# SyncE's order of issue in an attention kernel: weight and residual loads moved between the quarters of the exchange

## What is computed

```python
xn = layernorm(x)                                   # x: 2048 x 512, float32
q = (xn @ wq.T)                                     # 16 heads of 128 + 64 (rotary)
kv_lat, k_pe = split(xn @ wkv_a.T)                  # 128 latent, 64 rotary
q_lat = einsum(q_nope, wkv_b[:, :128]); q_pe, k_pe = rope(q_pe), rope(k_pe)
kv_cache = rmsnorm(kv_lat, kv_norm_w)
scores = (q_lat @ kv_cache.T + q_pe @ k_pe.T) * SCALE    # causal
out = softmax(scores) @ kv_cache @ wkv_b[:, 128:] @ wo.T
return x + out + xn @ ternary(weight).T + bias
```

## Time and profile before

| | |
|---|---|
| median of 3 runs | 1836.02 us (1835.36 to 1843.37) |
| the profiled execution | 1835.36 us, of it the span 1833.3 us |
| TensorE busy | 1715.3 us (94%) |
| VectorE, ScalarE, GpSimd busy | 1211.6, 849.0, 1009.4 us |
| granted TensorE clock, mean | 0.976 |
| SyncE's DMA queue, share of 16 engines | 43.7% |
| ScalarE's DMA queue | 15.8% |
| mean of all DMA traffic | 169 GB/s |

### The profile page before, as it was taken

One profiled execution on the slowest core, in us unless ns is written; L12 is line 12 of the kernel. 1 busy time (PEld: TensorE's weight loads), 2 busy tenths in 40 slices (PEclk: granted clock), 3 DMA queues, 4 the chain that ended last, 5 costly groups with the idle time before them and its releaser, 6 DMA issues. The chain is left out here.

```text
span 1833.3 us, 28210 instructions
## 1 busy us (share of the span) xinstructions
PE 1715.3 (94%) x9326; PEld 1446.9 (79%) x9326; DVE 1211.6 (66%) x2801; ACT 849.0 (46%) x1358; POOL 1009.4 (55%) x635
## 2 busy tenths in 40 slices
PE   6999789888999999999999999989999999999996
PEld 5887577667777777778888888878888888888885
DVE  4765476656666776666676666767677666766763
ACT  4554344443444544444544445434544544554442
POOL 4674544443555555555556556554646555565654
PEclk9888899989999999999999999999999999999998
DMA  6995355563766656756555545565756565655553
GB/s 196 371 331 212 107 148 171 161 216 110 202 172 167 160 151 179 210 167 172 150 149 154 157 132 149 170 188 151 191 132 151 146 164 130 158 153 130 149 129 109
DMA packets 127680, 309.12 MB, mean 169 GB/s; under 512 B 29554, under 2 KB 42099, under 8 KB 126388
## 3 DMA queue, kind: packets, MB, share of 16 engines
q1 hardware_dynamic: 98784, 227.04, 43.7%
q10 hardware_dynamic: 28756, 80.35, 15.8%
HBM read 113.28 MB, written 34.60 MB: 81 GB/s over the span
## 5 line engine op out<-in xcount | busy, mean ns | idle before, releaser
L1416 POOL TENSOR_TENSOR pT<-pT,pT_h 128x1024 fp32r<-128x1024 f32 x320 | 689.3, 2184 | 415.2 <-ACT pT_h L1322 413.2
L1196 DVE TENSOR_SCALAR_CACHE_REDUCE probs<-p_score 128x512 f32<-128x512 f32 (+3 forms) x640 | 382.2, 603 | 371.7 <-PE p_score L1124 225.9
L1301 ACT ACTIVATE probs<-probs,neg_max 128x128 f32<-128x128 f32 (+15 forms) x256 | 307.6, 1202 | 449.7 <-DVE neg_max L1202 399.4
L1322 ACT ACTIVATE pT_h<-pT 128x1024 fp32r<-128x1024 f32 x320 | 291.2, 963 | 241.9 <-PE p_out L1144 175.1
L1218 DVE STREAM_TRANSPOSE turned<-probs 128x1024 f32<-128x1024 f32 (+7 forms) x384 | 341.8, 916 | 40.6 <-ACT probs L1301 36.1
L1144 PE MATMUL p_out<-pT_h,V_h 128*128 128x256 f32 (+3 forms) x1024 | 301.3, 294 | 22.7 <-POOL pT L1416 22.6
L1144 PE MATMUL p_out<-pT,V_h 128*128 128x256 f32 (+3 forms) x1024 | 303.2, 296 | 0.0
L1144 PE MATMUL p_out<-pT_h,V_l 128*128 128x256 f32 (+3 forms) x1024 | 302.8, 296 | 0.0
L1124 PE MATMUL p_score<-Kp,qp_h 128*128 128x512 f32 (+3 forms) x640 | 236.8, 370 | 16.8 <-POOL qp_l L1408 16.7
L1124 PE MATMUL p_score<-Kn_h,q_h 128*128 128x512 f32 (+3 forms) x640 | 241.2, 377 | 3.5 <-DVE q_l L1241 3.0
L1124 PE MATMUL p_score<-Kn_l,q_h 128*128 128x512 f32 (+3 forms) x640 | 234.5, 366 | 0.0
(11 more groups left out here) (135 smaller groups left out, 2348.4 us busy)
## 6 DMA issues: line engine op xcount, KB each, us to landing
pT<-turned SPq DMA_DIRECT2D x384, 128.0 KB, 3.5
Wq<-wq_scr ACTq DMA_DIRECT2D x63, 512.0 KB, 4.4
Wv<-wv_scr SPq DMA_DIRECT2D x63, 512.0 KB, 3.8
pT<-turned SPq DMA_DIRECT2D x192, 112.0 KB, 3.8
pT<-turned SPq DMA_DIRECT2D x192, 96.0 KB, 2.6
pT<-turned ACTq DMA_DIRECT2D x128, 128.0 KB, 3.9
Wp<-wp_scr SPq DMA_DIRECT2D x31, 512.0 KB, 4.8
pT<-turned SPq DMA_DIRECT2D x192, 80.0 KB, 2.8
```

The source lines that it names most:

```text
L1196: dve.tensor_scalar(probs[row % ROW_RING][:, b * CW:b * CW + width], p_score[n % SCORE_RING][:, 0:width], SCALE, LOWEST, ALU.mult, ALU.max ...
L1301: act.activation(probs[row % ROW_RING][:, 0:width], probs[row % ROW_RING][:, 0:width], ACT.Exp, bias=neg_max[p][:, i:i + 1], scale=1.0, ac ...
L1322: act.activation(high.rearrange("p r t i q -> p r t (i q)"), low.bitcast(F32).rearrange("p r t i q -> p r t (i q)"), ACT.Copy).then_inc(p_ ...
L1416: pool.tensor_tensor(low.rearrange("p r t i q -> p r t (i q)"), low.bitcast(F32).rearrange("p r t i q -> p r t (i q)"), high.bitcast(F32). ...
```

## The change

Only the order of calls in SyncE's `slot(s)` is changed. No DMA is added, removed or resized, and each keeps its own waits. In every slot `load_rotary`, so far last, now stands between quarters 1 and 2 of the exchange and ahead of `load_next_v`. In the slots of a chunk change the second `store_half` and both `load_residual` now stand between the quarters.

```diff
                 if new:
                     store_half(new - 1, 0)
-                if new and new > 1:
-                    store_half(new - 1, 1)
                 if 1 <= s <= SLOTS:
-                    exchange(s - 1, (0, 1))
-                if s < 2 * H:
-                    load_next_v(s)
-                if new == 1:
+                    exchange(s - 1, (0,))
+                if new:
                     store_half(new - 1, 1)
                     load_residual(new, 0)
                 if 1 <= s <= SLOTS:
-                    exchange(s - 1, (2,))
-                if new and new > 1:
-                    load_residual(new, 0)
+                    exchange(s - 1, (1,))
                 if new:
                     load_residual(new, 1)
+                if opens_head(s) and head_of(s) % 2 and head_of(s) + 3 < HEADS:
+                    load_rotary(head_of(s) + 3)
+                if s < 2 * H:
+                    load_next_v(s)
+                if 1 <= s <= SLOTS:
+                    exchange(s - 1, (2,))
                 if s >= 2 * H:
                     load_next_v(s)
-                if opens_head(s) and head_of(s) % 2 and head_of(s) + 3 < HEADS:
-                    load_rotary(head_of(s) + 3)
```

## The result

The changed kernel takes 1869.18 us in the median (4 runs, 1862.61 to 1871.96), the kernel before in the same comparison 1839.69 us (4 runs): ratio 1.0155, 95% interval 1.0124 to 1.0186, or +29.5 us. It is slower, and it lies 13 us above the upper end of the predicted range. Sixteen further runs of the changed kernel have a median of 1868.7 us (1855.4 to 1874.8). In later comparisons the kernel before had medians of 1839.85 (29 runs), 1840.75 (23) and 1842.83 (28). One of these 28, at 3302.26 us, was a slow execution, and the intervals leave it out. So the execution profiled before (1835.36) was a favourable one; that of after took 1873.42 us, of it the span 1871.3. The two traces therefore differ by 38.0 us where the medians differ by 29.5.

The account below looks back on a forecast made before the run. Bound taken: exchange and `Wv` landing just in time in chunk 1, and tight chunk changes. Terms -1.0 + 2.9 + 0.8 + 1.0 + 3.3 + 1.7 = +8.7 us on 1835.36 gave 1844.1, median 1844.7 us, range 1837 to 1856.

Parts of the forecast that it names:

- The `Wp` loads: Chunk 0: issue hidden in a wait, -1.0 us; chunk 1: quarter 2 later, +2.9; slot 29: `Wv` later, +0.8.
- The row named as the sign of it: Chunk 1: TensorE's waits at L1156 were to go up; no size given.
- The second and third change: Slots 35 and 67: quarter 2 lands late behind store and residual, +3.3 us (0.2 to 5.7) and +1.7 (0 to 3.6).
- The wait: Slots 35 and 67: second residual half waits 5.9 us for the second store's landing, with quarter 2 behind it.
- The size: Quarter 2 lands 4.6 us late in slot 35 and 2.1 in slot 67, of which 1.3 and 0.4 are covered.
- The price per transfer that I held in hand: Chunk 1: upper bound of 2.1 us, the distance at which two such loads land under load.
- The first change: Slot 18: quarter 2 costs the loop 1.0 us, `Wv` some 4 us late, half swallowed; +1.0 us, bounds 0 and 4.
- The figure of 1.5 us: Chunk 1, `Wv` behind `Wp`: estimated time of 512 KB at 358 GB/s; 1.7 us was taken instead.
- The loop pays for the whole of `Wp`: Rival, odd slots 17 to 29: quarter 2 is 2.1 us late per slot, roundings 10.4 in all; 1852.2 us, chance 0.22.
- Hidden: Rival, whole kernel: every delay at its lower end, stores landing in 3 us; +0 to +4 us, about 1838, chance 0.23.
- faster: Rival, slot 18 and chunk 0: earlier loads end waits, -4 us at most, 1832; chance 0.05 of over 0.5% faster.

## Why the prediction was wrong

**What bounds the kernel** was read rightly: exchange and `Wv` arrive at their use in chunk 1, and the chunk changes are tight. The signs of the three terms for the chunk changes and of the sum for `Wp` came out, nothing was lost elsewhere in chunks 2 and 3, and slots 36 and 68 were the ones named. The times of issue were right to within 1 us too: in slot 18 `Wv` was expected 9.1 us after quarter 0 and went out at 8.8, in slot 35 quarter 2 was to be out at 11.5 and was at 10.7. What was wrong is what came between issue and landing. The loss was predicted at +8.7 and is +29.5.

**The `Wp` loads**, terms -1.0, +2.9 and +0.8, together +2.7: measured +5.7 (interval 1.7 to 9.8), so the term is in bounds. Measured from the start of quarter 0, quarter 2 lands in the odd slots 21 to 29 after 17.0 us in the mean (15.4 before), which is 1.6 later where 1.0 was taken, and `Wv` 1.4 later where 1.7 was taken. The whole set of traces agrees: the six with `Wp` last in the slot (before among them) have 15.0 to 16.1 us, the six with `Wp` ahead 16.5 to 17.9. In chunk 0 it lands no earlier, and the gain of 1.0 isn't seen. Where in chunk 1 the time is paid I can't show. The row named as the sign of it, the projection's wait for "issue" from 455 to 800 us, is 2.3 us in before and 10.5 with `Wp` moved:

```profile
PE p_result L1157 <- issue: 10.5, 8, 2.6
```

But the kernel with only the store moved in slots 35 and 67 has 11.0 there, with the old order in every slot of that stretch:

```profile
PE p_result L1159 <- issue: 11.0, 7, 2.4
```

and four others with `Wp` last in the slot have 3.3 to 6.6. A trace of one execution doesn't decide it.

**The second and third change**, +3.3 and +1.7: this is the step that failed. Slots 36 and 68 grew by 9.7 and 9.4 (7.0 to 9.7 and 5.5 to 9.4 over three kernels of that order). Three things were wrong in it.

- The wait. "The second residual half waits for its landing, 5.9 us" didn't occur: behind a store issued 5.0 us earlier, SyncE was still issuing quarter 1 when it had landed, and with the store done early and only the residual between, slot 36 still grew by 6.6.
- The size. I let quarter 2 be late by its later issue and a little sharing: 4.6 and 2.1 us. In truth 1.5 MB were put ahead of it in the same queue while the engines were full, and it was 8.3 and 7.8 us late, up to 2.8 us for each transfer (6.1 to 8.3 and 4.3 to 7.8 over the four kernels of that order). The price per transfer that I held in hand, up to 2.1 us, was near for one (1.8 and 1.9 measured) but was used nowhere in this step. Three times 2.1 would have given 6.3 and a term of +5.0.
- The clock. No term for it. A stall of 2.5 to 6.8 us in slot 36 went with a stretch at the lower level, which costs 1.8 to 2.9 us: 4.3 - 2.5 for store and one half, 6.6 - 4.1, 8.9 - 6.1 and 9.7 - 6.8 for the others. In slot 68 stalls of 3.7 to 7.2 us went with one that costs 1.5 to 2.2, and one of 2.2 us with none. Nor is the stall all that decides: with the residual on ScalarE's queue slot 36 has a stretch of 3.4 us although TensorE waits there only 2.0 and 0.3 us (1.2 in before).

Of the 14.1 us missing at these two slots (19.1 against 5.0), 5.1 are clock (2.9 and 2.2) and the rest is the size of the delay. By the means of the three kernels of that order (8.5 and 7.1) 10.6 us are missing.

**The first change**, +1.0, bounds 0 and 4: slots 17 to 19 take 7.7 to 10.3 us more in the four kernels that have the store, one or both residual halves and quarter 1 ahead of `Wv`. Here it was `Wv` that failed. "Some 4 us late, of which the 1.97 us that TensorE waits anyway swallow half" counts its issue and one transfer; it landed 10.2 us later against quarter 0. It landed 12.3 us after issue instead of 5.2, and its issue came 8.8 us after that of quarter 0, behind quarter 1 whose four DMAs had taken 4.43 us. One store ahead brings a wait of 3.3 us, and the whole set one of 8.7 to 10.7.

**The figure of 1.5 us.** From the 358 GB/s of the Trainium skill ("DMA: Bandwidth & Descriptors", "Specifications") 512 KB was an estimated 1.5 us. The runs show 1.8 to 1.9 us for the first transfer and 2.0 to 2.8 each for three, in a stretch where the full engines moved 207 GB/s. The ring order that the Trainium skill gives in the same page, "Queues, rings and completion order", spoke against the change, and the traces agree: in slot 35 the residual halves land 12.0 and 15.9 us after quarter 0, and quarter 2 behind them at 19.1.

**The rivals.** "The loop pays for the whole of `Wp`" doesn't fit as priced, though not by much (quarter 2 is 1.6 late, not 2.1, and this part lost 5.7 with an upper end of 9.8, not 10.2). "Hidden" and "faster" are out. What happened had been no rival: that the chunk changes alone cost 25 us. Their terms had upper bounds of 4, 5.7 and 3.6, 13.3 together, and even that was too low: quarter 2 was let be 7 us late at most and was 8.3, `Wv` was bounded without the queue ahead of it, and no bound held the clock.

**Left open.** What share of slots 17 to 31 is the change's and what the execution's. Where the remaining 4 of the 12.0 us with both halves between the quarters are spent. How the cost divides between the place in the queue and the shared engines, beyond the 1.7 us of earlier issue. What holds up one of quarter 1's issues. Why slot 68 varies more than slot 36 for the same order.

## What to carry to other kernels

Price a transfer that is moved ahead of a late one by its whole bytes, in the same queue, as many times as there are such transfers, and not by its issue: here 1.9 us for the first 512 KB and 6.1 to 8.3 for three. Ask first how much spare the transfer behind has; at the last two chunk changes it was 1.5 and 0.6 us. And add to a stall of TensorE what the lower clock costs: here 1.5 to 2.9 us on top of stalls of 2.5 to 7.2.

## What the runs showed that I had not expected

- One issue can take three times as long as its neighbours: quarter 1's four DMAs took 3.74 and 4.43 us behind a store and a residual half, quarter 0's 2.42 and 2.43, and quarter 2's, behind still more, 2.44 and 2.43.
- A transfer of 512 KB can take 12.3 us to land, and four small DMAs 10.0 us, when 1 to 1.5 MB have been put ahead of them.
- The same two loads cost slot 36 2.7 us from ScalarE's queue and 6.6 from between the quarters of SyncE's, and yet quarter 2 takes the same time from its issue to its last landing (9.3 and 9.2 us).
- 5.15 us of useless products in a stall of 6.7 us kept the granted clock at 1.00 (0.50 for 10.2 us without).
- The lengths of slots 17 to 31 together differ by up to 5.5 us between executions with one order of the queue, while slots 36 and 68 stay within 0.02 us where nothing was moved at their chunk change.
